# A vision transformer block with routed experts: dispatch in two parts, 13 expert groups from the first 12 tiles

## What is computed

```python
def _L0_ffn_ref(x, router_w, w1, b1, w2, b2):
    flat = x.reshape(-1, Cc)
    logits = flat @ router_w.T
    probs = jax.nn.softmax(logits.astype(jnp.float32), axis=-1)
    top_w, top_i = jax.lax.top_k(probs, K)
    top_w = (top_w / top_w.sum(-1, keepdims=True)).astype(x.dtype)
    out = jnp.zeros_like(flat)
    for e in range(E):
        w_e = jnp.sum(top_w * (top_i == e), axis=-1)[:, None]
        h = jax.nn.gelu(flat @ w1[e] + b1[e], approximate=False)
        out = out + w_e * (h @ w2[e] + b2[e])
    return out.reshape(B, T, Cc)
...
h = _L0_tok_ref(x, L0_tok_W)
h = h + _L0_attn_ref(_layernorm(h, axis=-1), L0_attn_W_attn, L0_attn_b_attn, L0_attn_W_o, L0_attn_b_o)
h = h + _L0_ffn_ref(_layernorm(h, axis=-1), L0_ffn_router_w, L0_ffn_w1, L0_ffn_b1, L0_ffn_w2, L0_ffn_b2)
```

## Time and profile before

| | us |
|---|---|
| median of 3 runs | 441.75 |
| lowest and highest | 441.44, 443.18 |
| time of the profiled execution | 444.34 |
| its span in the profile | 442.4 |

### The profile page before, as it was taken

How to read it: one execution, slowest core, us unless ns; L and a number is a source line. 1 busy time by engine, 2 the same in 40 slices (tenths; PEclk the granted TensorE clock), 3 DMA queues, 4 the chain that set the end, 5 groups by cost and what they waited for, 6 DMA issues and landing times.

```text
span 442.4 us, 14569 instructions
## 1 busy us (share of the span) xinstructions
PE 354.8 (80%) x5602; PEld 329.0 (74%) x5602; DVE 253.1 (57%) x638; ACT 219.8 (50%) x451; POOL 194.4 (44%) x236
## 2 busy tenths in 40 slices
PE   2788879998989899987622279799899898999920
PEld 2687779888989889877512169799899898999920
DVE  2566447787787766765349734455455455455417
ACT  3555648778888687753411024344344444344400
POOL 9005433446756664332630144465455455454220
PEclk9899999999999999975555579999999999999985
DMA  8757001444432333311006026621111111122039
GB/s 310 212 153 225 3 17 23 122 124 121 120 111 52 98 92 110 107 46 43 3 2 167 5 51 192 218 64 57 46 57 55 55 57 55 48 57 56 28 140 368
DMA packets 28654, 42.81 MB, mean 97 GB/s; under 512 B 12261, under 2 KB 18901, under 8 KB 28461
## 3 DMA queue, kind: packets, MB, share of 16 engines
q1 hardware_dynamic: 24460, 33.37, 25.0%
q0 software_dynamic: 4128, 8.50, 6.6%
...
## 4 chain that ended last, share of the span: by engine, by line
PE 45%; DVE 15%; issue 14%; POOL 10%; ACT 8%; DMA 6%; SPq 1%; POOLq 0%; DVEq 0%; ACTq 0%
PE PSA L1177 16%; PE PSA L1192 13%; PE PSA L958 4%; POOL XF L438 3%; POOL YP L450 2%; DMA REG<-xrows,KBR 2%; DMA W2l<-wqkv 2%; PE PSA L1015 2%; DVE H L947 2%; DVE REG L652 2%; PE PSA L1196 2%; PE PSA L1144 2%; DVE PTR L880 1%; PE PSA L990 1%; PE PSA L1041 1%
## 5 line engine op out<-in xcount | busy, mean ns | idle before, releaser
L1177 PE MATMUL PSA<-YT,W1h 128*128 128x128 f16 x774 | 79.4, 221 | 6.4 <-issue 4.7
L1177 PE MATMUL PSA<-YT,W1l 128*128 128x128 f16 (+1 forms) x516 | 76.6, 222 | 0.0
L482 POOL DMA_INDIRECT yrows<-KBR x43 | 43.9, 1022 | 69.0 <-DVE KBR L924 68.7
L1177 PEld LDWEIGHTS PSA<-YT,W1h 128*128 x774 | 64.6, 99 | 10.8 <-issue 5.5
L1192 PE MATMUL PSA<-W2h,PTR 128*128 x516 | 71.0, 246 | 0.3 <-DVE PTR L652 0.3
L638 ACT ACTIVATE PTR<-PSA 128x768 f32<-128x768 f32 x43 | 34.9, 811 | 69.3 <-PE PSA L1177 69.3
L1192 PE MATMUL PSA<-W2l,PTR 128*128 x258 | 63.5, 246 | 0.0
L477 POOL DMA_INDIRECT REG<-xrows,KBR x43 | 42.5, 987 | 43.0 <-DVE KBR L901 25.3
L643 ACT ACTIVATE PTR<-PTR 128x768 f16<-128x768 f32 x43 | 36.3, 843 | 46.2 <-PE PSA L1196 46.1
L652 DVE SCALAR_TENSOR_TENSOR PTR<-PTR 128x768 f16<-128x768 f32 x43 | 41.2, 958 | 25.9 <-ACT PTR L643 25.9
L958 PE MATMUL PSA<-W2h,REG 128*108 128x192 f16 x396 | 39.2, 261 | 17.7 <-DVE REG L652 17.6
...
## 6 DMA issues: line engine op xcount, KB each, us to landing
...
```

What stands on the lines that cost most here:

```text
L482: gp.indirect_dma_start(out=yrows, out_offset=bass.IndirectOffsetOnAxis(ap=TARGET[:, s:s + 1], axis=0), in_=YO[s % 2], in_offset=None).the ...
L1177: ins = nc.tensor.matmul(bank(2 * u + f // (FC // 2), 128, FC // 2 * ST_)[:, w:w + ST_], weights[a, c], YT[0:rows, at:at + ST_], start=k = ...
```

## The change

The dispatch is done twice. `EARLY` = 12 tiles hold 2592 token copies; at most 127 of each of the eight experts' can be left over, so at least 12.3, rounded to `FULL` = 13 groups, are full. These 13 groups come from tiles 0 to 11; the rest (what is left of those tiles, and tiles 12 to 21) fills 30 groups with padding. Every function of the routing now takes a part p.

- **First part.** Its selection, counts, slots and one-hot tables stand on VectorE behind the rounds 17, 18, 19 and 20 of attention, its ranks on PE in round 19, its table multiplication behind round 21. Its rows are written to `xfull`, and a copy to `xrows`.
- **The drain** is no longer three rounds; its functions stand, written out by hand, between the first expert steps of each engine.
- **Second part.** Its VectorE operations stand behind steps 2 to 10 of the experts, `ranks(1)` behind `down(3)` and `tables(1)` behind `down(8)` on PE.
- **Banks.** The drain and the second part use banks 6 and 7. The gathered rows are turned into bank 5 alone, and `down` writes bank 4 alone; the waits become `2 * s` and `s`. The turned rows go to `YM`, which lies over `QM`.
- **Gathers.** GpSimd issues those of steps 13 and 14 in round 10, 15 to 17 in rounds 10 to 12 behind the store, 18 to 20 in round 13, and then seven ahead as before.
- The weight pieces are two rounds earlier; the constants for routing are loaded at the start; the residual stream is written in two parts and read back in six; `G` lies in `WSTG`.

The core of the diff:

```diff
+EARLY = 12
+FULL = -(-(EARLY * TT * TOPK - E * (ST_ - 1)) // ST_)
+TILES = [(0, EARLY), (EARLY, NT)]
+COUNTED = [EARLY, NT]
+STEPS = [FULL, NS - FULL]
...
+        RELOADS = 6
+        READY = [(3, 6), (5, 10)]
+        LOADS = [n for p in range(2) for n in range(p * FULL, FULL + p * STEPS[1], LOADED)]
...
-            return range(max(0, 3 * i // 2), min(2 * PIECES, 3 * (i + 1) // 2))
+            return range(max(0, 3 * (i + 2) // 2), min(2 * PIECES, 3 * (i + 3) // 2))
...
+        def part(s):
+            return (0, s) if s < FULL else (1, s - FULL)
...
+        def sums_at(p):
+            return bank(7, ST_, CODES * STEPS[1]) if p else bank(1, ST_, 256 + TOPK * STEPS[0])[:, 256:]
...
+            def rows(p):
+                a, b = TILES[p]
+                sp.wait_ge(n2_lo, 2 * b)
+                sp.wait_ge(route[p], GATES[p])
+                for stored, to in ((rows_stored[0], xfull), (rows_kept, xrows), (rows_stored[1], xrows))[2 * p:2 + p]:
+                    for lo, hi in ((0, 96), (96, TT)):
+                        sp.dma_start(to.rearrange("(t p) c -> p t c", p=TT)[lo:hi, a:b, :],
+                                     RB[lo:hi, a * ROW:b * ROW].rearrange("p (t c) -> p t c", c=ROW)).then_inc(stored, 16)
...
+                if n == 0:
+                    gp.wait_ge(rows_kept, 16 * 2)
+                    gp.wait_ge(rows_stored[p], 16 * 2)
+                    gp.wait_ge(table[p], READY[p][0])
...
+            gp.wait_ge(n2_row, 18)
+            nc.gpsimd.memset(YM[CB:CX, :].rearrange("p (u c) -> p u c", u=2)[:, :, 3 * ST_:], S_X).then_inc(ones_set, 1)
+            gp.wait_ge(ones_set, 1)
+            norm2_low(16)
+            norm2_low(17)
+            y_low(21)
+            norm2_row(18)
+            norm2_row(19)
+            gather_rows(0)
+            gather_rows(1)
+            norm2_low(18)
+            norm2_low(19)
+            gather_rows(2)
+            gather_rows(3)
+            norm2_row(20)
+            norm2_row(21)
+            norm2_low(20)
+            norm2_low(21)
+            for s in range(4, FETCHED):
                 gather_rows(s)
...
             for s in range(NS):
+                if s == FULL - 3:
+                    for ahead in range(FULL, FULL + 2):
+                        gather_rows(ahead)
                 store_rows(s)
...
+                if s + FETCHED < FULL:
+                    gather_rows(s + FETCHED)
+                elif FULL - 3 <= s < FULL:
+                    gather_rows(s + 5)
+                elif s == FULL:
+                    for ahead in range(FULL + 5, FULL + FETCHED + 1):
+                        gather_rows(ahead)
+                elif FULL < s and s + FETCHED < NS:
...
+            def gaps(p):
+                a, b = TILES[p]
+                act.wait_ge(route[p], 11)
+                nc.scalar.activation(RT[:, NT + a:NT + b], RT[:, a:b], ACT.Exp, scale=1 / S_XW).then_inc(gap_exp[p], 1)
...
+                if i == 18:
+                    gaps(0)
+            norm2_out(16)
+            norm2_out(17)
+            y_hi(21)
+            norm2_hi(18)
+            norm2_hi(19)
+            y_out(21)
+            hidden(0)
+            norm2_out(18)
+            inverse_deviation(group(21))
+            norm2_out(19)
+            hidden(1)
+            norm2_hi(20)
+            norm2_hi(21)
+            hidden(2)
+            hidden(3)
+            norm2_out(20)
+            norm2_out(21)
+            hidden(4)
+            gaps(1)
+            for s in range(5, NS):
+                hidden(s)
...
+            def place(p):
+                done, tiles = count[p], COUNTED[p]
+                shape = [TT, tiles, E]
+                dve.wait_ge(count[p], 8)
+                dve.wait_ge(rank_mm[p], 2)
+                starts, ends = LIMIT[p][0:TT, E - 1:2 * E - 1], LIMIT[p][0:TT, E:2 * E]
...
+                dve.wait_ge(done, 10)
+                nc.vector.scalar_tensor_tensor(SLOTS[p], BEYOND[p], OUTSIDE, SLOTS[p], ALU.mult, ALU.add).then_inc(done, 1)
...
-                nc.vector.tensor_copy(YT[:, at:at + 3 * ST_], bank(6 + u, 128, 3 * ST_, F16)).then_inc(xt_done, 1)
-                nc.vector.tensor_copy(YT[0:CB, at + HIGH_B_ONES * ST_:at + 4 * ST_], bank(6 + u, CB, 3 * ST_, F16)[:, BOTH_B * ST_:]).then_inc(xt_done, 1)
+                nc.vector.tensor_copy(YM[:, at:at + 3 * ST_], bank(5, 128, 3 * ST_, F16)).then_inc(xt_done, 1)
...
-                nc.vector.tensor_scalar(YO[s % 2], bank(4 + s % 2, ST_, C), GATE[:, s:s + 1], None, ALU.mult).then_inc(y_done, 1)
-
+                nc.vector.tensor_scalar(YO[s % 2], bank(4, ST_, C), GATE[:, s:s + 1], None, ALU.mult).then_inc(y_done, 1)
...
+                if i == 17:
+                    choose(0, 0)
+                elif i == 18:
+                    dve.wait_ge(later_in, 16 * len(LATER))
+                    choose(0, 1)
+                elif i == 19:
+                    gates(0)
+                    dve.wait_ge(n1_lo, NT)
+                    tile_counts(0)
+                    place(0)
+                elif i == 20:
+                    dve.wait_ge(n1_mm, NT)
+                    place_high(0)
+                    place_code(0)
+                    dve.wait_ge(qk_mm, NT)
+                    dve.wait_ge(v_mm, NT)
+                    place_low(0, 0)
+                    for n in range(2):
+                        dve.wait_ge(v_in[n], V_IN * (6 - n))
+                    place_low(0, 1)
+            residual(20)
+            sources_full()
+            outputs(21)
+            stats2(20)
+            name_experts(0)
+            logits(16)
+            logits(17)
             rows_out(0)
             rows_out(1)
...
+                if s == 10:
+                    sources_rest()
+                    rows_out(FULL)
+                    rows_out(FULL + 1)
+                elif s != FULL - 4 and s + 4 < NS:
...
+                elif s == 8:
+                    place_low(1, 0)
+                    place_low(1, 1)
+                elif s == 9:
+                    name_experts(1)
...
-                need(pe, xt_done, 2 * s - 2)
+                need(pe, xt_done, 2 * s)
                 x = XR[s % XRS].bitcast(F16)
                 for n, at in enumerate(BLOCKS):
-                    ins = nc.tensor.transpose(bank(6 + s % 2, 128, 3 * ST_, F16)[:, n * ST_:(n + 1) * ST_], x[:, at:at + 128], IDH[:, :])
+                    ins = nc.tensor.transpose(bank(5, 128, 3 * ST_, F16)[:, n * ST_:(n + 1) * ST_], x[:, at:at + 128], IDH[:, :])
...
-                need(pe, y_done, s - 1)
+                need(pe, y_done, s)
...
+            tables(0)
+            project(20)
+            outputs(21)
+            norm2_transpose(22, 16)
+            norm2_transpose(22, 17)
+            router(22, 16)
+            router(22, 17)
+            pe.wait_ge(ptl_done, NT)
+            transpose_rows(0)
+            transpose_y(21)
+            pe.wait_ge(named[0], 4)
+            load_experts(0)
             pe.wait_ge(bias_in, 16 * 3)
...
+            pe.wait_ge(ones_set, 1)
+            pe.wait_ge(kh_done, 2 * NT)
+            pe.wait_ge(sub_done, NT)
+            pe.wait_ge(table[0], 1)
+            for f in range(FC):
+                up_addresses(expert[0], f)
+            up(0, 0, expert[0], None)
             transpose_rows(1)
...
+            project(21)
+            for f in range(FC):
+                up_addresses(expert[1], f)
+            transpose_rows(2)
+            up(1, 1, expert[1], None)
+            norm2_transpose(23, 18)
+            norm2_transpose(23, 19)
+            router(23, 18)
+            router(23, 19)
...
+                if s + 3 in LOADS:
+                    if s + 3 == FULL:
+                        pe.wait_ge(named[1], 3)
                     load_experts(s + 3)
                 if s + 2 < NS:
                     up(s + 2, u, expert[s + 2], expert[s])
-                if s + 4 < NS:
+                if s + 4 not in (FULL, FULL + 1) and s + 4 < NS:
                     transpose_rows(s + 4)
                 down(s, u, expert[s], expert[s + 3] if s + 3 < NS else None)
+                if s == 1:
+                    norm2_transpose(24, 20)
+                    norm2_transpose(24, 21)
+                    router(24, 20)
+                    router(24, 21)
+                elif s == 3:
+                    ranks(1)
+                elif s == 8:
+                    tables(1)
+                elif s == FULL - 3:
+                    transpose_rows(FULL)
+                    transpose_rows(FULL + 1)
```

577 lines of the change are left out of this document (344 added, 233 removed).

## The result

The changed kernel takes **503.9 us** (median of four runs, 498.3 to 508.2), the kernel before 442.5 us. I had said 486, with a range of 455 to 512, and slower with 93%. The difference to explain is thus 57 us.

What follows compares the result with a forecast made beforehand. PE, busy 80% of the span, was taken as the bound, with a 32.9 us hole between attention and experts. Terms -31.6, +13.9 and +62 gave +44.3 on 442.4: 486.7, so 486, range 455 to 512.

Steps and rivals of the forecast that it cites:

- the first `up`: First expert matmul after attention: starts at 226 instead of 257.6, -31.6 us (bounds 222 and 232).
- the start: From first `up` to t(0), start of the last matmul of `down(0)`: 24 us instead of 10.1, +13.9 us.
- steps 0 to 38: Expert loop from t(0) to t(38): 206.8 us against 144.9 before, +62 us.
- The ring: Expert loop: one row bank makes each transpose wait for the previous `rows_out`, 4.5 us a step instead of 3.64, +0.87.
- The single `down` bank: Expert loop: costs nothing, since `up` plus transpose cover the `gated` copy.
- VectorE's insertions: First routing in attention steps 17 to 20: 13 us of work, about 10 covered, so attention ends 3 us later.
- The stalls: Second table's hand-over, t(8) to t(14): steps of 9.7, 7.8 and 12.2 us, then three of 7.1 us each.
- the clock's 5: Expert loop: PE's clock falls while it waits 3 to 6 us, +5 us (bounds 0 and 12).
- The clock rival: Expert loop: granted clock stays low for much of it, 24 steps x 2.5 = +60, up to 545, half 515; 10%.
- The faster rival: Expert loop: row transpose does not wait because `rows_out` gets ahead; about 424 with none of the loss; 6%.

Runs made afterwards that it cites:

- e1: Kernel before, with gathered rows always transposed into bank 6, so each transpose waits for the copies of the step before: 477.2 us, ratio 1.077.
- e3: Changed kernel, with row transposes alternating between banks 5 and 6 from row 11 on: 475.0 us.
- e4: Changed kernel, one row bank, with `rows_out(s+4)` ahead of `hidden_lo(s+2)` on VectorE except in the first two and the hand-over rounds: 475.0 us.
- e2: Kernel before, with `down` always in bank 4, waiting for the gated copy of the step before: 444.8 us, ratio 1.003.
- e8: Changed kernel with row-transpose waits cured, second-table hand-over reordered, first gathers and expert register loads earlier, `norm2_out(19)` ahead of Ln and Exp: 440.6 us, ratio 0.993.
- e6: Changed kernel with both row-transpose cures, gathers of rows 13 to 18 earlier, and second-part experts named in round 8, not 9: 455.5 us.

## Why the prediction was right, and where it was off

The sum was 486.7 us against a measured span of 504.5: 9.4 for the first `up`, -1.6 for the start, 7.8 for steps 0 to 38 and 2.1 behind them. The members were the right ones but for one in the start, and no two large errors cancelled; nearly all terms were too small.

- **The ring was right**: +0.87 predicted, 0.84 to 0.91 in most plain steps of e1. The cause is shown by e1, e3 and e4. Steps 14 to 38 took 2.6 us more than I had: 1.5 since the plain step is 4.56 us (my own terms, 2.62 + 0.34 + 1.58, add up to 4.54, and I went on with 4.5), the rest since three load rounds add 2.3 us where I had 1.2.
- **The single `down` bank** costs nothing in the loop (e2), as said, and 1.2 us at its end, which I left out.
- **The first `up`** came at 235.4 instead of 226. Some 5 us of this are the profiled execution's own: its clock fell in the attention loop (rows in the last section), where e4, the same code up to there, had 1.00. In e3 and e4 the first `up` is at 230.8 and 229.4. What is left are two mis-sized terms. VectorE's insertions are 13.3 us as summed (13), but delay the start of the last `outputs` by 5 to 7 us (216.0 and 214.6 in e3 and e4, 209.3 and 209.7 in e1 and e2), not 3: less of them had cover than I counted. And from its end to `up` it takes 13.0 us, not 10.4: register loads on an idle PE are 2.9 us instead of 1.6 [the row at 235.43 above], and `y_low` and the two `norm2_row` ended some 1.2 us later than I had them.
- **The start** (24 predicted, 22.4 measured) had the right members: three table loads in a row and gather 4 behind the last norm. It did not have PE's router of tile 19, which waited 3.17 us at 247.22 and in e8, with the gathers moved ahead, left 18.5 us. The loads, ScalarE:

```profile
243.35 1.28 ACT L602 ACT_TABLE_LOAD   x1
244.64 0.30 ACT L602 ACTIVATE LNV<-VAR,EPSV 108x2 f32<-108x2 f32 x1
244.96 1.28 ACT L604 ACT_TABLE_LOAD   x1
...
246.80 1.28 ACT L724 ACT_TABLE_LOAD   x1
```

There are six after the first, as forecast. The Trainium skill, page "ScalarE: Activation LUTs", section on what ACT_TABLE_LOAD costs, adds 1.38 us of drain. This trace shows none at these three: each load starts 0.02 us after the activation before it has ended, and the activation behind it 0.01 us after the load. Both kernels begin with `preload_act_table_set("natural_log_exp_and_others")`, and up to the first Gelu the same Ln and Exp follow each other without a load (218.32 and 218.65 us); between two Gelus they took one each. Whether that call ahead of the Ln would save one of the three, 1.28 us, was not tried.

- **The stalls** were the right six, and mostly mis-sized by the same term. Predicted 9.7, 7.8, 12.2 and 3 x 7.1, measured 11.2, 10.3, 13.8, 8.0, 8.0, 9.5: 9.7 us more, for which my allowance was the clock's 5. After each of these waits `up` or `down` runs at half clock, as the earlier trace rows had shown for a shorter piece of work (stretches of 4 us in e6, columns as above; its wait of 6.48 us ends at 318.8):

```profile
308.00:312.00 4.00, 4.00 (x57) 3.66 (x54) 1.38 (x2) 1.66 (x2) 0.97 (x1) 1.00 0.08 29
...
316.00:320.00 4.00, 0.50 (x3) 0.24 (x3) 0.64 (x4) 0.00 (x0) 2.95 (x4) 0.50 0.21 50
320.00:324.00 4.00, 3.83 (x37) 3.84 (x38) 0.68 (x3) 0.00 (x0) 3.09 (x4) 0.50 0.33 74
```

  In the changed kernel `up` takes 3.2 to 3.3 us behind the three long waits (1.7 at full clock) and `down` 0.2 to 0.3 us more than its 1.6; behind the three shorter ones, where `up` has run already, `down` takes 2.7 to 3.0. So a stall costs its own length and then 1.1 to 1.8 us again, together some 9 us here. The largest of the other differences are the register loads ahead of `up(12)`, 2.15 us instead of 1.2, and the store ahead of the gather of rows 18, which took 1.55 us to issue, not 0.99.
- **The clock rival is refuted** for the loop: from t(14) to t(38) PE waited 0.67 us in each of 21 steps of 4.56, 1.3 to 1.8 us in the other three, and the granted clock was 1.00 from 360 to 484 us. The Trainium skill, page "TensorE: Matmul & The Clock Gate", section "A second HAM failure mode", tells of a kernel that cycles through PSUM banks, idles briefly between its groups of matmuls, and whose clock keeps falling and rising. Here, with such a pause in every step, it stayed up.
- **The faster rival** needed the copies ahead of the transpose. They were not, but e4 shows that one exchange of two lines would have made it so; with it alone the change still loses, 475 us, since the stalls and the start remain.
